# A four-layer sequence kernel: x also laid out by features, scales and denominators spread by DMA instead of TensorE transposes

## The reference, cut to what matters

```python
def _L0_attn_ref(x, ...):               # x: layernorm(x)
    y = xp[:, 0:Tv] * w_dw[:, 0] + xp[:, 1:Tv + 1] * w_dw[:, 1] + xp[:, 2:Tv + 2] * w_dw[:, 2]
    x = x + jnp.einsum('btd,ed->bte', y, w_pw)
    q, k, v = ...                       # 16 heads of 8; rotary on q and k; elu + 1
    num = jnp.einsum('bthd,bthdm->bthm', q_phi, kv_prefix)
    denom = jnp.sum(q_phi * k_prefix, axis=-1, keepdims=True)
    attn = num / (denom + 1e-06)
    gate = jax.nn.sigmoid(jnp.einsum('btd,ed->bte', delta, w_gate) + b_gate)
    x = x + gate * jnp.einsum('btd,ed->bte', attn, w_o)
    h = (x - mu) / jnp.sqrt(var + 1e-05) * ln_g + ln_b
    gw = jax.nn.softmax(jnp.einsum('btd,ed->bte', h, w_moe_gate), axis=-1)
    hid = jax.nn.silu(jnp.einsum('btd,efd->btef', h, w1) + b1)
    ffn = jnp.einsum('bte,bted->btd', gw, jnp.einsum('btef,edf->bted', hid, w2) + b2)
    return x + ffn
x = x + _L0_attn_ref(_layernorm(x, axis=-1), ...)
x = x + _L0_ffn_ref(_layernorm(x, axis=-1), ...)   # 8 experts, one per token, chosen by the largest of x @ gate_w.T
```

## Time and profile before

| | |
|---|---|
| median of 3 runs | 1480.37 us (1479.02 to 1481.9) |
| the profiled execution | 1480.5 us, span 1478.7 us |
| PE busy | 1266.4 us, 86% |
| DVE busy | 1013.0 us, 69% |
| ACT busy | 814.8 us, 55% |
| POOL busy | 712.6 us, 48% |
| granted PE clock, mean | 0.925 of full speed |

### The profile page before, as it was taken

How to read it: one execution, slowest core, us unless ns; L and a number is a source line. 1 busy time by engine, 2 the same in 40 slices (tenths; PEclk the granted TensorE clock), 3 DMA queues, 4 the chain that set the end, 5 groups by cost and what they waited for, 6 DMA issues and landing times. The chain is left out here.

```text
span 1478.7 us, 33273 instructions
## 1 busy us (share of the span) xinstructions
PE 1266.4 (86%) x10164; PEld 984.0 (67%) x10164; DVE 1013.0 (69%) x3390; ACT 814.8 (55%) x1703; POOL 712.6 (48%) x907
## 2 busy tenths in 40 slices
PE   2899999999986999999999965883988888739998
PEld 1566767676655877777777754773666666539997
DVE  3588888888735899999999984764566666522222
ACT  2355555556426776767777643552556555525554
POOL 3355565656420234343443542335566676426666
PEclk9799999999877999999999986996999999859999
DMA  1101011110102321212112205674111112168872
GB/s 62 40 30 39 31 33 33 31 37 28 45 13 62 69 54 44 64 41 62 40 48 59 73 16 142 196 202 146 27 44 47 49 55 44 44 233 300 266 264 69
DMA packets 70844, 117.53 MB, mean 79 GB/s; under 512 B 9746, under 2 KB 36635, under 8 KB 70768
## 3 DMA queue, kind: packets, MB, share of 16 engines
q1 hardware_dynamic: 58736, 93.49, 21.3%
q0 software_dynamic: 9856, 21.52, 4.6%
q10 hardware_dynamic: 2176, 1.61, 0.4%
HBM read 79.35 MB, written 29.88 MB: 74 GB/s over the span
## 5 line engine op out<-in xcount | busy, mean ns | idle before, releaser
L1159 DVE TENSOR_TENSOR m_Sl<-m_S,m_Sh 128x512 fp32r<-128x512 f32 x256 | 195.5, 769 | 23.3 <-ACT m_S L1076 20.6
L1076 ACT ACTIVATE m_S<-PS,W 128x512 f32<-128x512 f32 x256 | 174.7, 690 | 39.0 <-issue 33.1
L1071 ACT ACTIVATE m_Sh<-PS,W 128x512 fp32r<-128x512 f32 x192 | 132.9, 692 | 72.1 <-PE PS L996 64.5
L1459 POOL DMA_INDIRECT rows<-r_row,r_posi x128 | 131.2, 1025 | 36.2 <-issue 36.0
L761 DVE TENSOR_TENSOR am<-PS,C 128x512 f32<-128x512 f32 x192 | 119.6, 678 | 25.9 <-PE PS L454 25.4
L1693 PEld LDWEIGHTS PS<-f_wt,f_hid 128*128 128x128 f32 x960 | 121.3, 194 | 4.4
L1693 PE MATMUL PS<-f_wt,f_hid 128*128 128x128 f32 x960 | 121.5, 277 | 0.0
L1682 PE MATMUL PS<-f_xT,f_wt 128*128 128x256 f32 x480 | 121.2, 390 | 0.0
L965 POOL TENSOR_TENSOR m_oe<-m_oe 128x512 f32<-128x512 f32 x48 | 67.8, 1412 | 102.2 <-DVE m_oe L1140 101.7
L994 PE MATMUL PS<-m_HH,m_w1h 128*128 128x512 f32 x256 | 107.7, 421 | 7.1 <-DVE m_w1l L1112 4.7
L352 POOL TENSOR_TENSOR am<-am,C 128x512 f32<-128x512 f32 x64 | 81.6, 1275 | 54.8 <-ACT am L636 53.5
(11 more groups left out here) (237 smaller groups left out, 3127.2 us busy)
## 6 DMA issues: line engine op xcount, KB each, us to landing
f_wt<-wr SPq DMA_DIRECT2D x40, 578.0 KB
f_row<-rows SPq DMA_DIRECT2D x40, 260.0 KB
f_wt<-wr SPq DMA_DIRECT2D x40, 256.0 KB, 2.8
m_gb<-gates SPq DMA_DIRECT2D x8, 1024.0 KB, 7.7
m_raw<-gates SPq DMA_DIRECT2D x8, 1024.0 KB, 7.9
f_row<-rows SPq DMA_DIRECT2D x40, 132.0 KB, 2.1
mid<-f_res SPq DMA_DIRECT2D x20, 256.0 KB, 3.3
X<-x SPq DMA_DIRECT2D x16, 256.0 KB, 2.8
```

Source lines behind the costliest of these rows:

```text
L1071: nc.scalar.activation(Sh[:, n % 4, :], PS[:, n % 3, :], ACT.Silu, bias=w("b1")[:, n:n + 1]).then_inc(sh_ready, 1)
L1076: nc.scalar.activation(S[:, n % 3, :], PS[:, n % 3, :], ACT.Silu, bias=w("b1")[:, n:n + 1]).then_inc(s_ready, 1)
L1159: nc.vector.tensor_tensor(Sl[:, n % 4, :], S[:, n % 3, :], Sh[:, n % 4, :].bitcast(F32), ALU.subtract).then_inc(sl_ready, 1)
L1459: nc.gpsimd.indirect_dma_start(out=self.rows, out_offset=bass.IndirectOffsetOnAxis(ap=self.posi[:, u, t:t + 1], axis=0), in_=self.row[:, u ...
```

## The change

x is given twice, by tokens (into the still empty H, for the statistics alone) and by features (`xt`, into X and into xnT). SP writes the 512 values of 1/deviation to DRAM and reads them back to all partitions (`spread_rstd` into `rb`), and POOL multiplies `xnT` by it (`scale_x`). The mean isn't subtracted any more: the tap weights (and the router) are multiplied once by the centring matrix. For the second norm ACT writes scale and shift to DRAM and reads both rows back (`spread_scale2_out`, `spread_scale2_in` into `sb2`); POOL multiplies and adds (`scale_z`, `shift_z`) one step later, for the sequence e_, so `steps` has one more argument. One over the denominators is turned once (`turn_den`, one transpose in place of four), written to DRAM and read back eightfold (`rdT`). `keep_x1` moves from POOL to ACT, `keep_x2` is new there. `residual2` adds x2T to X by features; in `mixture` POOL adds X to the sum of the experts before it is turned back, ACT copies the turned result to X (`copy_back`, in place of DVE's `residual`), the router's matmuls read that sum by features (`pe_scores_columns`, no `pe_turn`, no `act_copy_xT`; DVE multiplies the logits by 1/deviation), and `ROUNDED` is empty: ACT makes all 16 `Sh`. The set-up block is merged into the first stage, with x loaded first and the zeroing of vm after the first `scale_x`. The last sequence still turns z on PE.

```diff
         @block.sync
+            def load_rows(b):
+                after_previous(sp, pw_psum, b)
+                sp.dma_start(xnT[:, 2:], xt[:, bass.ds(b * SEQ, SEQ)]).then_inc(xnT_in, 16)
+            def spread_rstd(b):
+                sp.wait_ge(rstd1_ready, b + 1)
+                after_previous(sp, rb_in, b, 16)
+                sp.dma_start(rstd_dram.rearrange("(p t) -> p t", p=P), rstd[:, :]).then_inc(rstd_out, 16)
+                sp.wait_ge(rstd_out, 16 * b + 16)
+                after_previous(sp, xn_ready, b)
+                sp.dma_start(rb[:, :], rstd_dram.unsqueeze(0).to_broadcast([P, SEQ])).then_inc(rb_in, 16)
...
         @block.gpsimd
+            def scale_x(b):
+                pool.wait_ge(rb_in, 16 * b + 16)
+                pool.wait_ge(xnT_in, 16 * b + 16)
+                nc.gpsimd.tensor_tensor(xnT[:, 2:], xnT[:, 2:], rb[:, :], ALU.mult).then_inc(xn_ready, 1)
+            def scale_z(b):
+                pool.wait_ge(x2_copied, b + 1)
+                pool.wait_ge(sb2_in, 16 * b + 16)
+                nc.gpsimd.tensor_tensor(x2c[:, :], x2c[:, :], sb2[:, 0, :], ALU.mult).then_inc(scaled, 1)
+            def shift_z(b):
+                pool.wait_ge(scaled, b + 1)
+                nc.gpsimd.tensor_tensor(x2c[:, :], x2c[:, :], sb2[:, 1, :], ALU.add).then_inc(z_ready, 1)
...
         @block.tensor
-            def turn_xn(b):
...
-            def turn_spread(b):
...
+            def turn_den(b):
+                pe.wait_ge(den_step, 2 * b + 2)
+                pe.wait_ge(v_ready, BATCHES if isinstance(b, int) and b >= BATCHES - 2 else b + 2)
+                nc.tensor.transpose(PS[:, 0, 0:P], den[:, :, :].rearrange("p a n -> p (a n)"), ident).then_inc(denT_psum, 1)
             def gate(b, u):
-                pe.wait_ge(rdT_ready, b + 1)
+                if since(b, 2):
+                    pe.wait_ge(lg_ready, b + (-1))
             def turn_x2(b):
-                    mm = nc.tensor.transpose(PS[:, 7, t * P:(t + 1) * P], x2T[:, t * P:(t + 1) * P], ident)
+                    tokens = x2T[:, t * P:(t + 1) * P] if final(b) else x2T[:, :].rearrange("d (p t) -> d t p", t=CT)[:, t, :]
+                    mm = nc.tensor.transpose(PS[:, 7, t * P:(t + 1) * P], tokens, ident)
...
         @block.scalar
+            def spread_den_in(b):
+                act.wait_ge(den_out, 16 * b + 16)
+                after_previous(act, wo_psum, b)
+                src = den_dram.rearrange("h t p -> h (t p)").unsqueeze(1).to_broadcast([HEADS, HD, SEQ])
+                act.dma_start(rdT[:, :], src).then_inc(rdT_in, 16)
...
                 if b is not None:
                     raw_scores(b, 1)
-                if n is not None:
-                    copy_xnT(n)
+                    keep_x1(b, u)
+                    copy_den(b)
+                    spread_den_out(b)
+                if e_ is not None:
+                    scale_h(e_)
+                if c_ is not None and not final(c_):
+                    keep_x2(c_)
                 if b is not None:
-                    spread_out(b)
                     raw_scores(b, 2)
+                    spread_den_in(b)
+                if c_ is not None and not final(c_):
+                    spread_scale2_out(c_)
                 if n is not None:
                     copy_x1(n, u)
-                if c_ is not None:
-                    normalise2(c_)
-                    scale_h(c_)
+                if c_ is not None and not final(c_):
+                    spread_scale2_in(c_)
                 if b is not None:
                     raw_scores(b, 3)
...
         @block.vector
             def residual2(b):
-                nc.vector.tensor_tensor(tokens(X, b), tokens(X, b), PS[:, 7, :].rearrange("p (c d) -> p c d", c=CT),
-                                        ALU.add).then_inc(x_added, 1)
+                dve.wait_ge(x2_step, 2 * b + 2)
+                dve.wait_ge(xt_in, 16 * b + 16)
+                nc.vector.tensor_tensor(columns(XT, b), columns(XT, b), x2T[:, :], ALU.add).then_inc(x_added, 1)
...
-        ROUNDED = (3,)
+        ROUNDED = ()
...
             def sums(b, e, v):
+                acc = oe[:, total_of(v), :]
+                if e == 1:
+                    pool.wait_ge(oe_ready, MOE * b + 1)
+                    nc.gpsimd.tensor_tensor(carrier[:, :], minus_half[:, :], minus_half[:, :], ALU.mult).then_inc(carried, 1)
+                    nc.gpsimd.tensor_tensor(acc, acc, XT[:, bass.ds(b * SEQ, SEQ)], ALU.add).then_inc(with_x, 1)
+                    pool.wait_ge(with_x, b + 1)
...
                 mm.then_inc(back_psum, 1)
+                routing.pe_scores_columns(pe, b, oe[:, total_of(v), :])
...
-                    if n == 0:
-                        route(routing.pe_turn, pe, r, v, tr)
-                    if n == 3:
-                        route(routing.pe_scores, pe, r, v, tr)
...
+            def copy_back(p):
+                act.wait_ge(back_psum, p + 1)
+                nc.scalar.activation(X[:, bass.ds(p * CT, CT), :], PS[:, 7, :].rearrange("p (c d) -> p c d", c=CT),
+                                     ACT.Copy).then_inc(x_ready, 1)
...
-                    if n == 8 and p is not None:
-                        residual(p)
```

More of the change, by code:

```diff
@@ L160, in wait_apart, with attention_front @@
     nc.vector.memset(scratch[:, 0:1], 0.0)
[L163 to L192, removed]
+def attention_front(nc, sems, X, w, c, PS, before, ones, minus_half, eps, scratch, H, LG, raw1, w1_in, w1t, x, xt, wsmall, consts, W, C,
+                    rstd_dram, z_dram, den_dram):
     with ExitStack() as ctx:
@@ L386, in steps @@
                     mask_last(b, 0)
-                    keep_x1(b, u)
+                if e_ is not None:
+                    scale_z(e_)
+                if n is not None:
+                    scale_x(n)
+                if b is None and n is not None and n == 0:
+                    nc.gpsimd.memset(vm[:, :, :, :, :], 0.0).then_inc(zeroed, 1)
+                if b is not None:
                     mask_last(b, 1)
+                if e_ is not None:
+                    shift_z(e_)
                 if c_ is not None:
-                    inverse_deviation(c_, ln2_stats, mv2, ve2, ve2_done, rstd2, rstd2_ready, shift2, shift2_ready, z_ready, negated2)
+                    inverse_deviation2(c_)
                 if b is not None:
@@ L556, in steps @@
                     update_state(b, u, 1)
+                    turn_den(b)
                     weigh(b, u, 1)
@@ L831, in steps @@
                     mask_scores(b, 3)
-            make_taps()
             stages(dve, steps)
@@ L1079, in one @@
                 for n in range(N):
-                    if n == 1:
-                        route(routing.act_copy_xT, act, r, v, tr)
+                    if n == 8 and p is not None:
+                        copy_back(p)
                     if n == 7:
@@ L1495, in pe_scores, with pe_scores_columns @@
             mm = nc.tensor.matmul(self.bank[:, t * EXPERTS:(t + 1) * EXPERTS], self.xT[:, t * P:(t + 1) * P], self.router,
+                                  start=True, stop=True)
+        mm.then_inc(self.lg_psum, 1)
+    def pe_scores_columns(self, pe, b, columns):
+        nc = self.nc
+        after_previous(pe, self.lg_ready, b)
+        for t in range(CT):
+            mm = nc.tensor.matmul(self.bank[:, t * EXPERTS:(t + 1) * EXPERTS], columns[:, t * P:(t + 1) * P], self.router,
                                   start=True, stop=True)
```

316 lines of the change are left out of this document (181 added, 135 removed).

## The result

The changed kernel takes 1501.42 us (median of 4 runs, 1499.99 to 1503.7), the kernel before beside it 1481.13 (4 runs, 1479.02 to 1482.9): 1.0139 of it, 95% interval 1.0118 to 1.016. It is slower, where I had forecast 1456 us.

A forecast was written before the change was run, and what follows sets the result against it. The front was taken as bound by a loop through PE and DVE, the mixture by PE's matmuls except around batch seams. +9 - 3 - 8 - 19 - 3.5 = -24.5 on 1480.5 gave 1456 us; own range 1446 to 1465, 8-in-10 range 1431 to 1475.

The forecast's parts named there:

- PE's transposes: Front: removing them takes 1.35 us a step off PE, taken as worth 0 in the steady part, bounds 0 and 1.35.
- the front's steady part: Front's steps: lock +1.85 less DVE's waits 0.67, on average +0.7 us a step; +9 us, bounds -9 and +25.
- the three signs: Prediction wrong if close's line keeps 0.69 us, PE's clock falls every step (up to 0.9 us each), or ACT stands between chunks.
- The lock: Front: DVE instructions with two SBUF operands stand still behind POOL's scale_z and scale_x; +1.85 us a step, bounds 0 and 2.56.
- DVE's two waits: Front: DVE's waits for the load of X (0.39 us) and the spread denominators (0.28) go; up to 0.67 us a step.
- PE waits over 1 us for tile 1: Front: sign expected in the changed kernel's timeline, PE waiting over 1 us for tile 1's mask.
- Start: Kernel start: set-up block, barrier and one turn through PE and ACT go, a DRAM round trip comes; -3 us, bounds 0 and -5.
- End of the front: Last two steps: turn_z, a wait for ACT's h and turn_spread go ahead of the gate's matmuls; -8 us, bounds -3 and -12.
- Mixture: Batch seam: router's transposes and waits go, up(0) waits for ACT's S; 1.25 us a batch, -19 over 15, last batch -3.5.
- Slower: Rival, chance 0.1: ACT's wait for scale and shift landing in DRAM delays tile 3's scores; 1486 us if landing takes 7.2 us.
- Nothing gained: Rival, chance 0.05: the round trips eat the gain, 1480 us.
- mixture gains only the transposes: Rival, chance 0.2: ACT gets late with four more Sh and copy_back; mixture gives -6 instead of -19, 1469 us.

The follow-up runs named there:

- e8: Kernel before with three of four transposes left out of each of turn_xn, turn_spread and turn_z in the loop's twelve steps; 1.0024 of the kernel before.
- e10: Changed kernel plus six idle PE transposes behind the logits near the step's end, not where PE waits for the denominators; 1.0096 of the kernel before.
- e3: Changed kernel with ACT's spread_scale2_in moved behind raw_scores of tile 3, nothing else; 1.0112 of the kernel before.
- e9: Changed kernel plus six idle PE transposes ahead of update_state of tile 1, and spread_scale2_in behind raw_scores of tile 3; 0.99 of the kernel before.
- e11: Changed kernel with POOL's scaling behind tile 1's mask, H loaded a step earlier, spread_scale2_in behind raw_scores of tile 3, no idle transposes; 0.9923 of the kernel before.

## Why the prediction was wrong

*What failed* is one step: "About every second step is longer, with the granted clock at 0.57 [...]; I keep that as it is", and with it PE's transposes "worth nothing" between the bounds 0 and 1.35 us. At a given clock they are worth nothing (e8's steps at the full clock take 23.4 us, as before), but the clock was not given: less PE work and a new wait made it fall in every step and for longer. That a removal can cost time was outside both bounds. In the sum, the front's steady part stood at +9 with +25 as its end, and measured +32.4 us. The part that I had summed up was about right: 13 steps of 24.0 to 24.5 us, as e10 has them at the full clock, are 312 to 319 us, +1 to +7 on the 311.4 of before. The other 25 to 31 us are the clock's, which is an estimate from those steps. The clock rows give a like size: 0.96 less 0.86 over 311 us of the old front is 31 us of PE's full-speed work that has to be made up, also an estimate, for PE is not waited for in all of it.

*What I had seen and mis-placed:* of the three signs that were to show the prediction wrong, one came, "if PE's clock falls in every step", but with it stood "that adds up to 0.9 us to a step". That price came from a low stretch of 3 us that lay beside DVE work. In the changed kernel the long ones lie over `pointwise`, where DVE waits, and a step with ten low microseconds is on average 2.4 us longer than one with three. The other two signs, `close`'s line at 0.69 us and ACT standing between chunks, did not come.

*The lock.* Right in mechanism, place and order of instructions, though `phi` k and the addition do not end where a POOL multiplication ends, as the text's own sign has it, but 0.55 us later, as its sum has it. Of its size +1.85 us were forecast and 1.35 measured: POOL gets in as soon as `phi` q is through, while DVE's multiplication out of PSUM, 0.67 us, runs beside it and pays nothing. A fast step was to cost +1.2 us net; by e10's it costs +0.6 to +1.1.

*DVE's two waits:* the one for the denominators went, as forecast (13.1 us in 12 between 70 and 425 us before, none after). The one for x did not: 4.4 us in 4, before 3.7 in 7. *PE waits over 1 us for tile 1:* 0.79 or 0.88 us for the denominators and 0.2 behind them, so about 1 us.

*Start* -3.4 (forecast -3). *End of the front* -3.9 + 0.5 = -3.4 (forecast -8): `logits` still waits for ACT and the bank, only the transposes went. *Mixture:* a full batch went from 26.00 to 25.17 us, -0.84 where -1.25 was forecast; up(0) waits 0.74 us for the last `S`, forecast 0.9. There are twelve such batches and not fifteen, -10 us; around them the stage loses 4, and it gives -5.7 instead of -19. Of the -3.5 us for the last batch nothing shows: from the last `back` to the end it is -0.4. No wait for `Sl` is left, right. Its PE row at the seam, beside the earlier trace rows:

```profile
635.52 0.50 PE L1080 MATMUL PS<-m_HH,m_w1h 128*128 128x512 f32 x1 [0.74 <-ACT m_S L1164]
```

*The rivals.* "Slower" was given 0.1 and came, but by another road: the landing of scale and shift takes 4.1 us (median), not the 6.8 from which it decides, and moving that wait changed nothing (e3). With the clock kept up it may be real (e9, whose front doesn't show it). "Nothing gained" and "mixture gains only the transposes" name the sizes better than my forecast did, for other reasons. And the range called my own, 1446 to 1465, is not what the bounds give one term at a time: the front alone takes the sum from 1438 to 1472. Even so 1501 lies outside.

*Settled:* the loss lies in the front, PE work put into the wait undoes it and brings the clock up, and it does so with the lock, the transfers and POOL's work as they were. *Shown only in part:* how the loss divides between the missing transposes, the lock and the transfers. The missing transposes alone cost the kernel before 4 us (e8, interval from 0 to 7); without the lock and the two waits the changed kernel stays within 4 us of the old front (e11, 365.2 against 361.4); together it is 29 us. That these don't add up is measured. Why just this combination puts the low stretch over `pointwise` is argued from the timelines, not tried.

The Trainium skill, TensorE: Matmul & The Clock Gate, section "A second HAM failure mode: psum-queue depth-cycling", tells of a kernel in which short idle moments between groups of matmuls let the clock swing between its levels; the traces here agree, with a mean of 0.86 at PE waits of 1.0 us and less.

## What to carry to other kernels

Where PE is near its bound and its granted clock is not 1.00 throughout, ask of every removed matmul and every added wait what they do to the clock, and where in the step a low stretch would then fall: here three low microseconds cost 0.9 us where DVE had other work, and seven more cost 2.4 where DVE waited. When a change that takes work away makes a kernel slower, a few idle transposes put into the wait can tell in one run whether it is the clock. And when one limit goes, look at once for the transfers that were just in time for the old pace.

## What was unexpected of the hardware

PE was busy for 322.6 of 350 us, waited 1.0 us at the longest in the front's steady part, and yet ran at the lower level for over a quarter of the time (mean 0.86). Chips differed by 22 to 37 us in stages that the edits don't touch, and the one with the quickest made the whole kernel 2% faster. And a multiplication on POOL of 1.27 us took 1.72 and 1.54 us beside DVE instructions: the standing still is on both sides.
